# Attention kernel on one core: softmax denominators turned through 32x32 blocks before they are inverted

## The chip, the cores and the metric

The program runs on one core of a Trainium2 chip. The metric is the device time of one launch, in microseconds. PE is TensorE, DVE VectorE, ACT ScalarE, POOL GpSimd, SP the queue that issues most DMAs.

## What is computed

`x` is (2, 2048, 512), fp32. A layer norm of it goes into a causal attention with 16 heads of 32 and ALiBi slopes, and into a top-1 mixture of 8 experts; both are added to `x`. The change touches only the end of the softmax:

```python
attn = jnp.einsum('bhqd,bhkd->bhqk', q, k) / math.sqrt(HEAD_DIM)
attn = attn + alibi_bias(seq_len, N_HEADS)[None] + causal_mask(seq_len)[None, None]
attn = jax.nn.softmax(attn, axis=-1)
y = jnp.einsum('bhqk,bhkd->bhqd', attn, v)
...
x = x + _L0_attn_ref(xn, W_qkv, W_o) + _L0_ffn_ref(xn, wg, W, b)
```

The kernel divides late: it forms the unnormalised products with v and the row sums of the exponentials, and multiplies the one by the inverse of the other.

## The kernel before

Four stages follow each other, each in a block of its own that all engines enter and leave together: projection and routing (0 to about 360 us), attention (to 1560), the experts (to 1724), and the output product with the sums (to 1825). The change is in attention, function `attend`.

**Tiling.** Two batch rows of 16 heads make G = 8 groups of four heads (HG = 4), each head on 32 of the 128 partitions. A group's 2048 queries are QC = 4 chunks of 512. A round is one chunk with one block of 128 keys, up to the diagonal: 4 + 8 + 12 + 16 = NR = 40 rounds in a group. The last rounds of the chunks (LAST_ROUND) are 3, 11, 23 and 39.

**PE, lines 1131 to 1151.** PE goes through the rounds in pairs. For each pair it first issues eight score matmuls (L1082, four heads by two rounds; on diagonal rounds a small mask matmul at L1085 follows each), and between them the matmuls of the maxima (L1050): one max unit behind each score, four units in a round in the steady state. Here this is called a score stretch. Then come the value products (L1126) and row sums (L1117, L1093) of the pair of rounds before, here a value stretch, written to `y_ps` and `den_ps`, the two banks of `acc_ps`. The row sums use an all-ones matrix with 32 columns, so that the 32 partitions of a head all hold the same denominators. Each round's values raise `pv_done`. At the first round of a chunk the value stretch waits until the accumulators of the chunk before have left (L1101). Between two groups no value stretch stands between rounds 0-1 and 2-3: their scores form one double stretch.

**Maxima.** The row maxima are found ahead of the exponentials, some of them in the group before, by a hand-made plan (`PLAN_FIRST` for the first group, which has more units in a round, `PLAN_MID` for the six groups in the middle, `PLAN_LAST` for the last, which has none after round 14). DVE takes each max unit out of one of three banks of `max_ps` (L940, on the diagonal L936); PE needs a bank again three units later. FOLD, TURN and SPLIT make a chunk's maxima into rows: DVE L948, PE L1070, ACT L997, DVE L955; then SP stores them (L832).

**ACT.** Exponentials, L1021, out of three banks of `score_ps`. Two rounds after a chunk's last one ACT copies both banks of `acc_ps` into `acc_sb` (`leave`, L1005) and raises `accs_left`.

**DVE's inversion.** `den_sb` is the half of `acc_sb` with the denominators. `INVERT_AT` puts a quarter of it (128 columns) at the end of DVE's work for each of the rounds LAST_ROUND + 3 to + 6 (L972), in place. Chunk 3's fall into the next group's rounds 2 to 5.

**POOL.** Adds pairs of `probs` (L917) for the row sums, and multiplies `y_sb` by `den_sb` (`normalise`, L897) ahead of the pair that `Y_BEFORE_PAIR` names (pairs 1, 2, 5 and 9 of the 12). SP stores the product (L837); in the first group it stands ahead of the load of the second group's q and k (L804) in SP's order:

```python
y_out(g, 0)
max_rows(g, 2, half)
load(g + 1, 1 - half)
```

After the last group each engine runs the inversion of the last chunk with nothing else to do, and the block ends when the last `y` is stored.

Of the kernel before, what the change touches and what calls it, by code (L numbers as in the profile page):

```python
# [8 lines left out]
F32 = mybir.dt.float32  # L9
# [3 lines left out]
ACT = mybir.ActivationFunctionType  # L13
# [3 lines left out]
P = 128  # L17
B, S, D = 2, 2048, 512
H, DH = 16, 32
E = 8  # L20
N = B * S
CH = 512
# [8 lines left out]
QC = S // CH  # L31
# [19 lines left out]
NR = len(ROUNDS)  # L51
# [10 lines left out]
NPAIR = len(PAIR_OF) // 2  # L62
PAIR_LAST = {p: r for r, p in PAIR_OF.items()}
LAST_ROUND = [max(r for r, (cc, _) in enumerate(ROUNDS) if cc == c) for c in range(QC)]
# [73 lines left out]
def plan_of(g, last):  # L138
# [3 lines left out]
    if isinstance(g, int) and g == 0:  # L142
# [4 lines left out]


LEAVE_AT = {(LAST_ROUND[c] + 2) % NR: ((LAST_ROUND[c] + 2) // NR, c) for c in range(QC)}
QUARTERS = 4  # L150
INVERT_AT = {(LAST_ROUND[c] + 3 + k) % NR: ((LAST_ROUND[c] + 3 + k) // NR, c, k)
             for c in range(QC) for k in range(QUARTERS)}

Y_BEFORE_PAIR = {min([p for p in range(NPAIR) if PAIR_LAST[p] > (LAST_ROUND[c] + 3 + QUARTERS) % NR] or [NPAIR]):
                 ((LAST_ROUND[c] + 3 + QUARTERS) // NR, c) for c in range(QC)}


class Memory:
# [3 lines left out]
def wait_past(eng, sem, count):  # L162

    if not isinstance(count, int) or count > 0:
        eng.wait_ge(sem, count)
# [570 lines left out]
def attend(nc, m):  # L736
# [6 lines left out]
    with ExitStack() as c:  # L743
        sb = lambda n, s, d: c.enter_context(nc.sbuf_tensor(n, s, d))
# [9 lines left out]
        max_lo = sb("max_lo", [HG * TPC, 2, P], F32R)  # L754
        acc_sb = sb("acc_sb", [P, 2, 2, CH], F32)
        y_sb, den_sb = acc_sb[:, :, 0], acc_sb[:, :, 1]
        score_ps = pb("score_ps", [P, S_BANKS, CH], F32)
        max_ps = pb("max_ps", [P, M_BANKS, CH], F32)
        acc_ps = pb("acc_ps", [P, 2, CH], F32)
# [36 lines left out]
        with nc.Block() as block:  # L796
# [86 lines left out]
            @block.gpsimd  # L883
            def _(pool):
                nc.gpsimd.iota(token[:], [[P, NT]], base=0, channel_multiplier=1).then_inc(token_made, 1)  # L885
                pool.wait_ge(token_made, 1)

                def place_tokens(k):

                    for t in range(k * SCATTERS, (k + 1) * SCATTERS):  # L890
                        pool.indirect_dma_start(m.slot_token_d, bass.IndirectOffsetOnAxis(ap=m.slot_cell[:, t:t + 1], axis=0),
                                                token[:, t:t + 1], None).then_inc(tokens_stored, 16)

                def normalise(g, cc):
                    n = g * QC + cc
                    pool.wait_ge(inverted, (n + 1) * QUARTERS)
                    nc.gpsimd.tensor_tensor(y_sb[:, cc % 2], y_sb[:, cc % 2], den_sb[:, cc % 2], ALU.mult).then_inc(y_done, 1)  # L897

                def step(g, half, first, last):
                    exps, used = base(pool, g, NSU), base(pool, g, NPAIR)  # L900
                    for p in range(NPAIR + 1):
                        if p in Y_BEFORE_PAIR:
                            back, cc = Y_BEFORE_PAIR[p]
                            if not (first and back):
                                normalise(g - back, cc)
                        if p == NPAIR:
                            break
                        if first and 1 <= p <= NT // SCATTERS:
                            place_tokens(p - 1)
                        r1 = PAIR_LAST[p]  # L910
                        s0, s1 = (r1 - 1) % P_SLOTS, r1 % P_SLOTS
                        if not (first and p < 2):

                            pool.wait_ge(pair_used, used + (p - 1))
                        for hh in range(HG):
                            pool.wait_ge(exp_done, exps + (r1 * HG + hh + 1))
                            nc.gpsimd.tensor_tensor(pair_sum[:, p % 2, hh], probs[:, s0, hh], probs[:, s1, hh],  # L917
                                                    ALU.add).then_inc(pair_added, 1)

                groups(pool, step)  # L920
                normalise(G - 1, QC - 1)
                pool.wait_ge(tokens_stored, 16 * NT)

            @block.vector
            def _(dve):
                nc.vector.memset(neg_max[:], 0.0).then_inc(max_blank, 1)
                dve.wait_ge(max_blank, 1)
                part = part_max[:].rearrange("p (h i) k -> p h i k", h=HG)

                def take_max(u, bank, units):  # L930
                    i, kc, hh = MAX_UNITS[u]
                    w = min(CH, (i + 1) * P - kc * CH)
                    dve.wait_ge(max_scored, units + (u + 1))
                    if kc == i // TPC:

                        nc.vector.tensor_tensor_reduce(max_ps[:, bank, 0:w], max_ps[:, bank, 0:w], m.mask_row[:, CH - w:CH],  # L936
                                                       1.0, LOWEST, ALU.add, ALU.max,
                                                       part_max[:, hh * QT + i, kc:kc + 1]).then_inc(max_taken, 1)
                    else:
                        nc.vector.tensor_reduce(part_max[:, hh * QT + i, kc:kc + 1], max_ps[:, bank, 0:w], AX.X,  # L940
                                                ALU.max).then_inc(max_taken, 1)

                def fold(g, cc, units):

                    n = g * QC + cc
                    dve.wait_ge(max_taken, units + (OF_CHUNK[cc][-1] + 1))
                    wait_past(dve, max_turned, n)
                    nc.vector.tensor_reduce(neg_max[:, 0:HG * TPC].rearrange("p (h i) -> p h i", h=HG),  # L948
                                            part[:, :, cc * TPC:(cc + 1) * TPC, 0:cc + 1], AX.X, ALU.max,
                                            negate=True).then_inc(neg_done, 1)  # L950

                def low_rows(g, cc, bank):

                    dve.wait_ge(max_hi_done, g * QC + cc + 1)
                    nc.vector.tensor_tensor(max_lo[:, cc % 2], max_ps[0:HG * TPC, bank, 0:P], max_hi[:, cc % 2].bitcast(F32),  # L955
                                            ALU.subtract).then_inc(max_lo_done, 1)

                def maxima(events, banks, g, units):

                    for dg, kind, n in events:  # L960
                        if kind == UNIT:
                            take_max(n, banks[dg, kind, n][0], units[dg])
                        elif kind == FOLD:
                            fold(g + dg, n, units[dg])
                        elif kind == SPLIT:
                            low_rows(g + dg, n, banks[dg, TURN, n][0])

                def invert(g, cc, k):

                    dve.wait_ge(accs_left, g * QC + cc + 1)  # L970
                    quarter = den_sb[:, cc % 2, bass.ts(k, CH // QUARTERS)]
                    nc.vector.reciprocal(quarter, quarter).then_inc(inverted, 1)  # L972

                def step(g, half, first, last):
                    events, banks = plan_of(g, last)
                    units = base(dve, g, NMU), None if last else base(dve, g + 1, NMU)
                    for r in range(NR):
                        maxima(events[r], banks, g, units)
                        if r in INVERT_AT:
                            back, cc, k = INVERT_AT[r]  # L980
                            if not (first and back):
                                invert(g - back, cc, k)

                maxima(PLAN_BEFORE[0], BANKS_BEFORE, 0, (0, None))
                groups(dve, step)
                for k in range(QUARTERS):
                    invert(G - 1, QC - 1, k)

            @block.scalar
            def _(act):  # L990
# [9 lines left out]
                def leave(g, cc):  # L1000

                    act.wait_ge(pv_done, g * NR + LAST_ROUND[cc] + 1)

                    wait_past(act, y_stored[cc % 2], 16 * (g * (QC // 2) + cc // 2))
                    nc.scalar.activation(acc_sb[:, cc % 2], acc_ps[:], ACT.Copy).then_inc(accs_left, 1)  # L1005

                def step(g, half, first, last):
                    events, banks = plan_of(g, last)
# [25 lines left out]
            def _(pe):  # L1034
# [62 lines left out]
                def probs_of(g, r, exps):  # L1097
                    cc, jb = ROUNDS[r]
                    if jb == 0:

                        wait_past(pe, accs_left, g * QC + cc)  # L1101
                    pe.wait_ge(exp_done, exps + (r + 1) * HG)

                def has_row_sums(r):
# [370 lines left out]
```

## Time and profile before

| | us |
|---|---|
| median of 3 runs | 1824.9 |
| lowest, highest | 1824.75, 1836.62 |
| the profiled execution | 1827.11 |
| its span | 1825.4 |
| PE busy | 1687.3 (92%) |
| DVE busy | 1104.7 (61%) |
| ACT busy | 785.2 (43%) |
| POOL busy | 675.6 (37%) |

The profiled execution's own time is 1.7 us above its span and 2.2 us above the median. Busy shares are unions of the instructions of an engine; PE's matmuls overlap each other, so its 92% doesn't say how close it is to its best. The mean granted clock of TensorE over the span is 0.97.

### The profile page before, as it was taken

To read this page: it belongs to the slowest core of one execution; us is meant where nothing else is said; L and a number is where in the kernel's file an instruction comes from. 1 tells how busy PE (TensorE), PEld (TensorE's weight loads), DVE (VectorE), ACT (ScalarE), POOL (GpSimd) and SP (SyncE) were. 2 spreads that over 40 slices of the span, in tenths; PEclk is the share of its full clock that TensorE was granted. 3 is DMA by queue.
4 is the path that set the end of the run, shared out by engine and by line. 5 is a ranking of instruction groups with operands and counts; after the bars stand their busy time and mean duration, and the time that the engine had idled before them with its cause. 6 is when DMAs were issued, how large, how long until landed. Compare 5 with 4: busy or idle time off the path is not lost. (4 is left out here: it accounts for less than half of the span.)

```text
span 1825.4 us, 27949 instructions
## 1 busy us (share of the span) xinstructions
PE 1687.3 (92%) x9970; PEld 1015.6 (56%) x9971; DVE 1104.7 (61%) x2484; ACT 785.2 (43%) x1575; POOL 675.6 (37%) x643
## 2 busy tenths in 40 slices
PE   5999999579899999999999999999999999689898
PEld 4777777444444444454545444444554443568686
DVE  5333333468677767776876876876777710634466
ACT  2222222024354555564655555565556555411111
POOL 4500000006572552553444454355256256132360
PEclk9999999769999999999999999999999999899899
DMA  6655554744604503602701800900900500355596
GB/s 219 210 185 179 197 189 160 159 77 84 106 8 92 98 13 73 117 7 60 136 7 39 156 8 20 175 8 8 180 16 7 197 7 6 133 161 166 176 393 231
DMA packets 96927, 203.59 MB, mean 112 GB/s; under 512 B 10908, under 2 KB 28348, under 8 KB 91164
## 3 DMA queue, kind: packets, MB, share of 16 engines
q1 hardware_dynamic: 87592, 178.56, 37.8%
q0 software_dynamic: 9216, 23.47, 4.1%
q8 instruction: 72, 1.18, 0.3%
q14 instruction: 47, 0.39, 0.1%
HBM read 122.46 MB, written 79.01 MB: 110 GB/s over the span
## 5 line engine op out<-in xcount | busy, mean ns | idle before, releaser
L1021 ACT ACTIVATE probs_sb<-score_ps 128x512 f32<-128x512 f32 (+3 forms) x1280 | 606.8, 546 | 503.2 <-PE score_ps L1085 196.0
L917 POOL TENSOR_TENSOR pair_sum<-probs_sb 128x512 f32<-128x512 f32 x384 | 480.2, 1283 | 598.7 <-ACT probs_sb L1021 493.1
L940 DVE TENSOR_REDUCE part_max<-max_ps 128x1 f32<-128x512 f32 x768 | 474.2, 680 | 250.4 <-PE max_ps L1050 247.8
L1050 PE MATMUL max_ps<-k_aug,q_aug 104*128 104x512 f32 (+3 forms) x1280 | 534.1, 427 | 54.1 <-DMA q_aug<-q_rows_d 22.8
L1082 PE MATMUL score_ps<-q_aug,k_aug 106*128 106x512 f32 (+3 forms) x1280 | 494.3, 393 | 18.7 <-DMA q_aug<-max_lo 9.8
L1082 PEld LDWEIGHTS score_ps<-q_aug,k_aug 106*128 106x128 f32 x1280 | 243.7, 191 | 183.1 <-issue 112.1
L1050 PEld LDWEIGHTS max_ps<-k_aug,q_aug 104*128 104x128 f32 x1280 | 251.1, 197 | 160.7 <-DVE part_max L940 82.1
L1126 PE MATMUL acc_ps<-probs_sb,v_sb 128*32 128x512 f32 (+3 forms) x2560 | 294.6, 539 | 0.0
L936 DVE CUSTOM_DVE_ANT_0 max_ps<-max_ps,mask_row 128x384 f32<-128x384 f32 (+3 forms) x512 | 238.9, 515 | 57.1 <-PE max_ps L1050 55.6
L972 DVE RECIPROCAL acc_sb<-acc_sb 128x128 f32<-128x128 f32 x128 | 119.7, 940 | 76.6 <-ACT acc_sb L1005 76.6
L1126 PEld LDWEIGHTS acc_ps<-probs_sb,v_sb 128*32 128x32 f32 x2560 | 73.2, 110 | 117.4 <-issue 97.4
L613 DVE SCALAR_TENSOR_TENSOR st_lo<-group_ps,st_hi 128x512 fp32r<-128x512 f32 x64 | 44.3, 692 | 139.2 <-ACT st_hi L660 139.2
L1085 PE MATMUL score_ps<-mask_kq,ident_bf 128*128 128x128 bf16 x512 | 118.9, 232 | 0.0
L723 PE MATMUL group_ps<-xT_hi,w_hi 128*128 128x512 f32 x256 | 102.0, 398 | 0.0
L1093 PE MATMUL acc_ps<-pair_sum,ones 128*32 128x512 f32 x768 | 101.3, 599 | 0.0
L723 PE MATMUL group_ps<-xT_lo,w_hi 128*128 128x512 f32 x256 | 101.3, 396 | 0.0
L723 PE MATMUL group_ps<-xT_hi,w_lo 128*128 128x512 f32 x256 | 101.2, 395 | 0.0
L660 ACT ACTIVATE st_hi<-group_ps 128x512 fp32r<-128x512 f32 x64 | 38.3, 598 | 141.1 <-PE group_ps L723 141.1
L885 POOL IOTA token<- 128x32 int32 x1 | 0.2, 154 | 256.4 <-POOLq L346 256.4
L1117 PE MATMUL acc_ps<-probs_sb,ones 128*32 128x512 f32 (+3 forms) x1024 | 93.7, 438 | 0.0
L1085 PEld LDWEIGHTS score_ps<-mask_kq,ident_bf 128*128 128x128 bf16 x512 | 50.0, 98 | 76.5 <-issue 58.4
L1224 POOL DMA_INDIRECT rows<-xn_d,slot_token x39 | 37.3, 957 | 97.6 <-PE turn_ps L1321 90.2
(173 smaller groups left out, 1737.8 us busy)
## 6 DMA issues: line engine op xcount, KB each, us to landing
k_aug<-k_hi_d SPq DMA_DIRECT2D x14, 1024.0 KB
q_aug<-q_hi_d SPq DMA_DIRECT2D x14, 1024.0 KB
slot_y_d<-y_rows SPq DMA_DIRECT2D x39, 256.0 KB, 2.0
xn_d<-xn SPq DMA_DIRECT2D x8, 1024.0 KB, 5.5
q_hi_d<-st_hi SPq DMA_DIRECT2D x32, 256.0 KB, 3.4
q_lo_d<-st_lo SPq DMA_DIRECT2D x32, 256.0 KB, 3.7
k_hi_d<-st_hi SPq DMA_DIRECT2D x32, 256.0 KB, 2.5
k_lo_d<-st_lo SPq DMA_DIRECT2D x32, 256.0 KB, 2.8
```

The lines of the kernel that those rows point to most:

```text
L723: last = nc.tensor.matmul(group_ps[:, n % BANKS], lhs, rhs, start=(k == 0 and p == 0), stop=(k == KC - 1 and p == 2))
L917: nc.gpsimd.tensor_tensor(pair_sum[:, p % 2, hh], probs[:, s0, hh], probs[:, s1, hh], ALU.add).then_inc(pair_added, 1)
L936: nc.vector.tensor_tensor_reduce(max_ps[:, bank, 0:w], max_ps[:, bank, 0:w], m.mask_row[:, CH - w:CH], 1.0, LOWEST, ALU.add, ALU.max, part ...
L940: nc.vector.tensor_reduce(part_max[:, hh * QT + i, kc:kc + 1], max_ps[:, bank, 0:w], AX.X, ALU.max).then_inc(max_taken, 1)
L972: nc.vector.reciprocal(quarter, quarter).then_inc(inverted, 1)
L1021: nc.scalar.activation(probs[:, r % P_SLOTS, hh, off:CH], score_ps[:, (r * HG + hh) % S_BANKS, off:CH], ACT.Exp).then_inc(exp_done, 1)
L1050: nc.tensor.matmul(max_ps[:, bank, 0:w], q_aug[0:ROW_MAX, half, hh, i * P:(i + 1) * P], k_aug[0:ROW_MAX, half, hh, kc * CH:kc * CH + w], s ...
L1082: last = nc.tensor.matmul(score_ps[:, u % S_BANKS, off:CH], k_aug[0:ROWS, half, hh, jb * P:(jb + 1) * P], q_aug[0:ROWS, half, hh, cc * CH ...
L1085: last = nc.tensor.matmul(score_ps[:, u % S_BANKS, off:off + P], m.ident_bf[:], m.mask_kq[:], start=False, stop=True)
L1093: last = nc.tensor.matmul(den_ps[hh * DH:(hh + 1) * DH, :], m.ones[:], pair_sum[:, p % 2, hh], start=start, stop=False)
L1117: nc.tensor.matmul(den_ps[hh * DH:(hh + 1) * DH, off:CH], m.ones[:], probs[:, r % P_SLOTS, hh, off:CH], start=jb == 0, stop=r == LAST_ROUN ...
L1126: last = nc.tensor.matmul(y_ps[hh * DH:(hh + 1) * DH, off:CH], v_sb[:, half, jb, hh * DH:(hh + 1) * DH], probs[:, r % P_SLOTS, hh, off:CH] ...
```

## The change

The inversion has three steps in place of four quarters. Step 0, at round LAST_ROUND + 2, transposes `den_ps` straight out of PSUM in blocks of 32 x 32 into `den_sb`: after it partition i of a head holds query 32 s + i in each column of block s. Step 1, a round later, takes one column of each of the 16 blocks (16 elements a partition, step 32) and inverts those into `den_fold`. Step 2, another round later, reads `den_fold` with each element repeated 32 times, transposes again in 32 x 32 blocks, and leaves the inverses of all 512 queries on all 32 partitions of a head in `den_sb`. Each step waits for the one before it; step 0 also waits for `pv_done` of the chunk's last round and for `y_done` of two chunks earlier. ACT copies only the `y_ps` bank, 512 columns. POOL waits for `accs_left` too, and goes ahead of pairs 1, 2, 4 and 8. PE, at the first value products of a chunk, waits for step 0 of the chunk before in addition to `accs_left`.

```diff
-QUARTERS = 4
-INVERT_AT = {(LAST_ROUND[c] + 3 + k) % NR: ((LAST_ROUND[c] + 3 + k) // NR, c, k)
-             for c in range(QC) for k in range(QUARTERS)}
+INVERT_STEPS = 3
+INVERT_AT = {(LAST_ROUND[c] + 2 + k) % NR: ((LAST_ROUND[c] + 2 + k) // NR, c, k)
+             for c in range(QC) for k in range(INVERT_STEPS)}
...
+        den_fold = sb("den_fold", [P, CH // DH], F32)
...
-                    pool.wait_ge(inverted, (n + 1) * QUARTERS)
+                    pool.wait_ge(accs_left, n + 1)
+                    pool.wait_ge(inverted, (n + 1) * INVERT_STEPS)
...
-                    dve.wait_ge(accs_left, g * QC + cc + 1)
-                    quarter = den_sb[:, cc % 2, bass.ts(k, CH // QUARTERS)]
-                    nc.vector.reciprocal(quarter, quarter).then_inc(inverted, 1)
+                    n = g * QC + cc
+                    if k == 0:
+                        dve.wait_ge(pv_done, g * NR + LAST_ROUND[cc] + 1)
+
+                        wait_past(dve, y_done, n - 1)
+                        nc.vector.transpose(den_sb[:, cc % 2], den_ps).then_inc(inverted, 1)
+                    elif k == 1:
+
+                        dve.wait_ge(inverted, n * INVERT_STEPS + 1)
+                        nc.vector.reciprocal(den_fold[:], den_sb[:, cc % 2].rearrange("p (s d) -> p s d", d=DH)[:, :, 0]).then_inc(
+                            inverted, 1)
+                    else:
+                        dve.wait_ge(inverted, n * INVERT_STEPS + 2)
+                        nc.vector.transpose(den_sb[:, cc % 2].rearrange("p (s d) -> p s d", d=DH),
+                                            den_fold[:].unsqueeze(2).to_broadcast([P, CH // DH, DH])).then_inc(inverted, 1)
...
-                for k in range(QUARTERS):
+                for k in range(INVERT_STEPS):
                     invert(G - 1, QC - 1, k)
...
-                    nc.scalar.activation(acc_sb[:, cc % 2], acc_ps[:], ACT.Copy).then_inc(accs_left, 1)
+                    nc.scalar.activation(y_sb[:, cc % 2], y_ps, ACT.Copy).then_inc(accs_left, 1)
...
                         wait_past(pe, accs_left, g * QC + cc)
+                        wait_past(pe, inverted, (g * QC + cc) * INVERT_STEPS - INVERT_STEPS + 1)
```

## Rows read from the trace of the kernel before

**Rows 1.** Busy time by engine, one middle group of attention (stretch first, then us)

```profile
713.00:854.00 141.00, 136.69 (x936) 69.73 (x930) 103.73 (x248) 79.64 (x168) 65.04 (x52) 1.00 0.35 66
```

**Rows 2.** Waits in that group: waiter <- releaser: us, times, longest

```profile
ACT probs_sb L1021 <- POOL pair_sum L917: 17.1, 6, 3.5
...
PE max_ps L1050 <- DVE part_max L936: 1.8, 3, 0.7
...
PE max_ps L1050 <- DVE part_max L940: 1.3, 2, 0.8
...
PE score_ps L1082 <- ACT probs_sb L1021: 0.6, 2, 0.5
PE max_ps L1050 <- DVE max_lo L955: 0.3, 1, 0.3
```

**Rows 3.** DVE's timeline, a middle group (start us, us, instructions)

```profile
874.18 2.48 DVE L940 TENSOR_REDUCE part_max<-max_ps 128x1 f32<-128x512 f32 x4 [0.63 <-PE max_ps L1050]
876.58 0.94 DVE L972 RECIPROCAL acc_sb<-acc_sb 128x128 f32<-128x128 f32 x1
877.44 2.41 DVE L940 TENSOR_REDUCE part_max<-max_ps 128x1 f32<-128x512 f32 x4
```

**Rows 4.** ACT's timeline: its copy at the start of rounds 6-7 of that group

```profile
873.54 1.03 ACT L1005 ACTIVATE acc_sb<-acc_ps 128x1024 f32<-128x1024 f32 x1 [1.82 <-PE acc_ps L1126]
```

**Rows 5.** PE's timeline: rounds 4-5 of that group, and the next stretch's wait

```profile
867.10 0.50 PE L1082 MATMUL score_ps<-q_aug,k_aug 106*128 106x512 f32 x1
...
871.65 0.39 PE L1050 MATMUL max_ps<-k_aug,q_aug 104*128 104x256 f32 x1 [0.62 <-DVE part_max L936]
871.97 0.64 PE L1117 MATMUL acc_ps<-probs_sb,ones 128*32 128x256 f32 x8
...
878.12 0.50 PE L1050 MATMUL max_ps<-k_aug,q_aug 104*128 104x512 f32 x1 [0.55 <-DVE part_max L940]
```

**Rows 6.** PE's timeline: rounds 30-31 of that group

```profile
958.25 0.50 PE L1082 MATMUL score_ps<-q_aug,k_aug 106*128 106x512 f32 x1
...
962.27 1.06 PE L1126 MATMUL acc_ps<-probs_sb,v_sb 128*32 128x512 f32 x8
```

**Rows 7.** Groups of instructions by line: busy us, mean ns, idle before

```profile
L940 DVE TENSOR_REDUCE part_max<-max_ps 128x1 f32<-128x512 f32 x768 | 474.2, 680 | 250.4 <-PE max_ps L1050 247.8 <-issue 2.3
...
L972 DVE RECIPROCAL acc_sb<-acc_sb 128x128 f32<-128x128 f32 x128 | 119.7, 940 | 76.6 <-ACT acc_sb L1005 76.6
...
L1005 ACT ACTIVATE acc_sb<-acc_ps 128x1024 f32<-128x1024 f32 x32 | 32.8, 1025 | 40.4 <-PE acc_ps L1126 40.4
...
L665 ACT ACTIVATE st_v<-group_ps 128x512 f32<-128x512 f32 x32 | 19.1, 597 | 70.7 <-PE group_ps L723 70.7
...
L488 DVE RECIPROCAL inv<-root 128x4 f32<-128x4 f32 x8 | 1.4, 178 | 43.3 <-ACT root L637 43.3
```

**Rows 8.** PE's timeline: rounds 14-15 of the same group

```profile
904.21 0.50 PE L1082 MATMUL score_ps<-q_aug,k_aug 106*128 106x512 f32 x1 [0.45 <-ACT probs_sb L1021]
```

**Rows 9.** SP's timeline in the first group

```profile
432.44 0.36 SPq L837 DMA_DIRECT2D y_d<-acc_sb  x1
```

**Rows 10.** DVE's timeline in the first group

```profile
430.12 0.94 DVE L972 RECIPROCAL acc_sb<-acc_sb 128x128 f32<-128x128 f32 x1
```

**Rows 11.** PE's timeline in the first group: one wait for DVE

```profile
427.87 0.50 PE L1050 MATMUL max_ps<-k_aug,q_aug 104*128 104x512 f32 x1 [0.71 <-DVE part_max L940]
```

**Rows 12.** PE's timeline in the first group: its wait for the second group's rows

```profile
481.43 0.47 PE L1050 MATMUL max_ps<-k_aug,q_aug 104*128 104x128 f32 x1 [3.45 <-DMA q_aug<-q_rows_d]
```

**Rows 13.** All engines' timeline at the end of attention

```profile
1551.62 1.02 ACT L1005 ACTIVATE acc_sb<-acc_ps 128x1024 f32<-128x1024 f32 x1 [5.06 <-PE acc_ps L1126]
1552.67 3.39 DVE L972 RECIPROCAL acc_sb<-acc_sb 128x128 f32<-128x128 f32 x4 [42.16 <-ACT acc_sb L1005]
1556.14 1.26 POOL L897 TENSOR_TENSOR acc_sb<-acc_sb 128x512 f32<-128x512 f32 x1 [14.47 <-DVE acc_sb L972]
...
1560.38 14.80 PE L1311 MATMUL turn_ps<-ident,w_nat 128*128 128x128 f32 x110 [8.82 <-PEq L796]
```

More of the change, by code:

```diff
@@ L149 @@
 LEAVE_AT = {(LAST_ROUND[c] + 2) % NR: ((LAST_ROUND[c] + 2) // NR, c) for c in range(QC)}
-QUARTERS = 4
-INVERT_AT = {(LAST_ROUND[c] + 3 + k) % NR: ((LAST_ROUND[c] + 3 + k) // NR, c, k)
-             for c in range(QC) for k in range(QUARTERS)}
-Y_BEFORE_PAIR = {min([p for p in range(NPAIR) if PAIR_LAST[p] > (LAST_ROUND[c] + 3 + QUARTERS) % NR] or [NPAIR]):
-                 ((LAST_ROUND[c] + 3 + QUARTERS) // NR, c) for c in range(QC)}
+INVERT_STEPS = 3
+INVERT_AT = {(LAST_ROUND[c] + 2 + k) % NR: ((LAST_ROUND[c] + 2 + k) // NR, c, k)
+             for c in range(QC) for k in range(INVERT_STEPS)}
+Y_BEFORE_PAIR = {min([p for p in range(NPAIR) if PAIR_LAST[p] > (LAST_ROUND[c] + 2 + INVERT_STEPS) % NR] or [NPAIR]):
+                 ((LAST_ROUND[c] + 2 + INVERT_STEPS) // NR, c) for c in range(QC)}
 class Memory:
```

## The prediction

> **What bounds the kernel now.** I read the page first, then the windows of attention, the waits of one group, and the timelines of PE, DVE and ACT inside it. Attention takes about two thirds of the time and repeats with a period of 141 us; in one such group PE is busy for 136.7 of 141 us, DVE for 103.7, ACT for 79.6 [rows 1]. So PE sets the period, and only what makes PE stop can give time back. The reader should see in the waits which stops there are: PE stood for DVE's maxima 1.8 us (3 times), 1.3 (2 times) and 0.3 (once), and for ACT's exponentials 0.6 us [rows 2]. 4.0 us of 141 is the most direct part of what a lighter DVE and ACT can return.
>
> DVE is not slow on average, yet it is within a score stretch. A max unit of 512 columns costs it about 0.60 us in sequence (2.48 us for four, overlapping), and PE issues one with each score about every 0.50 us (eight in 4.02 us [rows 6]). With three banks DVE can fall behind by two units before PE stops. Where a reciprocal stands between the fourth and the fifth unit it adds 0.86 us (876.58 to 877.44) [rows 3], and PE's last max of the stretch starts after a stop of 0.55 us; in rounds 4-5 it is 0.62 us [rows 5]. Each chunk has four reciprocals. Those of its first and third round lie inside stretches; the other two lie at the end of a stretch, where PE goes on to value products, and cost nothing.
>
> What a stop costs is more than its idle row. Rounds 4-5 and rounds 30-31 hold the same matmuls (eight scores of 512 columns, four max units of 512 and four of 256), and only the first has a reciprocal inside: 867.10 to 871.97 is 4.87 us [rows 5], 958.25 to 962.27 is 4.02 us [rows 6]. The difference is 0.85 for an idle row of 0.62, so I add 0.23 us a stop.
>
> **What the change removes and adds on DVE.** Removed: 128 reciprocals of 128 columns, 940 ns each, 119.7 us in all [rows 7], 3.76 us a chunk. Added a chunk: one reciprocal of 16 columns and two transposes of 512. The reciprocal's price follows from two sizes: 178 ns for 4 columns, 940 for 128, so 6.15 ns a column and 0.25 us for 16 [rows 7]. No row shows a transpose. The nearest is DVE's pass over 512 columns of PSUM, 680 ns (L940 [rows 7]); I take 0.69 us for both, since each moves 512 columns once. Below, the trace has no DVE pass over 512 columns that takes less than 0.60 us in sequence (2.41 us for four [rows 3]); above, the dearest column in the trace is the reciprocal's, 6.15 ns, which would make 3.3 us. Between ends so far apart I go by the L940 row, as a transpose does no arithmetic. A chunk then costs DVE 0.69 + 0.25 + 0.69 = 1.63 us, 2.1 less; over 32 chunks DVE loses about 68 us of work. Most of it is under PE's work and worth nothing; what counts is where the pieces lie.
>
> The third step reads one word 32 times over and the second steps by 32 words. The Trainium skill (Vector Engine (DVE) Microarchitecture Reference, Measured stream behaviour on trn2) says that a port keeps its full rate only for runs of at least two adjacent words, and gives 1.7 to 2.5 ns a column for streams that jump at every element. No run here shows that for a transpose; by it the third step would be an estimated 0.3 to 0.8 us longer, and as that step lies under value products the sum would change by that once, at the end of attention.
>
> **Where the new steps lie, in a middle group.** Chunks 0, 1 and 2 end in an odd round L. Step 0 follows the max units of round L+2, the end of a stretch, and waits for `pv_done` of L, which comes with the end of the value stretch behind it: ACT's copy, which waits for the same, starts at 873.54 [rows 4], and DVE's first unit of the next stretch would start at 874.18 [rows 3]. Behind the waiting step stand only that unit and its followers, which PE has not issued yet, so the wait is free; the transpose runs to about 874.25 and delays them by 0.1 us. Step 1 lies inside that stretch and adds 0.2 us in sequence where there were 0.86. Step 2 lies at the stretch's end, hidden under the value products, where 0.94 us of reciprocal is hidden now. The stretch after that has nothing.
>
> - Second stretches (rounds 4-5, 8-9, 16-17, 28-29): the three stops for L936, 1.8 us [rows 2], plus 3 x 0.23, go: 2.5 us.
> - First stretches: rounds 6-7, 0.55 [rows 5] + 0.23, less the 0.3 that the new steps add: 0.5. Rounds 26-27, the 0.3 for max_lo + 0.23, less about 0.15: 0.35. Rounds 14-15 are held by ACT, whose copy of 1025 ns comes ahead of the exponentials (PE stops for 0.45 us [rows 8]); 512 columns cost it 597 ns [rows 7], so 0.4 comes back.
> - Chunk 3's steps fall into the double stretch of rounds 0-3, step 0 after round 1 and step 1 after round 2: 0.94 us inside it, as before. Step 1 and step 0 cost 0.2 and 0.7 in sequence, and step 0 comes where DVE has room before its next unit; I take 0.25.
>
> Together 2.5 + 1.5 = 4.0 us a group, 24 us for six groups.
>
> **The added waits of PE and POOL.** PE's wait for step 0 is read at the value products, more than 4 us into the stretch [rows 5, 6]; step 0 ends 0.9 us into it. Free, with 3 us to spare. POOL's `normalise` comes a pair earlier for three chunks of four, and its inputs are ready by then; it stops waiting for the fourth reciprocal. SP's stores follow earlier. None of this is late for anyone. If that cover went, POOL's 1.3 us would hold back pair sums, for which ACT already waited 17.1 us a group as the last of its conditions [rows 2].
>
> **The last group.** Rounds 0 to 9 as before: 0.25 + 0.85 + 0.5 + 0.75 = 2.3 us. After that there are no maxima and DVE is idle; ACT's shorter copies give 0.4 and 0.3. At the very end nothing covers: ACT's copy at 1551.62, the reciprocals from 1552.67 for 3.39 us, POOL at 1556.14, and PE's first expert work at 1560.38 [rows 13]. The new chain starts at 1551.62 beside ACT's copy and takes 0.69 + 0.25 + 0.69 plus two handovers of some 0.05: POOL starts at 1553.4, 2.7 us sooner. Sum 5.7 us.
>
> **The first group.** SP can only load the second group's rows after `y` of chunk 0 is stored, at 432.44, and after eight stores of maxima rows that follow 0.4 us later [rows 9]. PE later waits 3.45 us for that load [rows 12]. Now `y` would be out well before, since chunk 0's inverses are ready by round 7 in place of round 9. The maxima rows then wait for `max_lo` of chunk 2 alone. It starts at the end of a reciprocal, 430.12 + 0.86 [rows 10]; that reciprocal goes (0.9), and the stretches before it shrink by 0.45 and by 0.71 [rows 11] + 0.23, so it is ready near 428.9. The load is issued 3.9 us sooner. PE itself arrives at its wait some 2.7 us sooner, so the wait persists and the whole 3.9 us is passed on. Chunk 2's two stretches behind it give 0.4 and 0.9. Sum 5.2 us.
>
> **Sum.** 24 + 5.7 + 5.2 = 34.9 us. On the profiled execution's span of 1825.4 (own time 1827.11, 2.2 above the median) that is 1790.5; on the median of 1824.9 it gives 1790.0.
>
> **The rivals.**
> - *Transposes at half the pass rate.* A 4-byte word through a 32 x 32 block may take two passes: 1.2 to 1.3 us each. Nothing in the trace speaks for or against. Step 0 then delays the three first stretches by 0.55 more and adds as much in the double stretch; those gains vanish (1.5 to about 0 and -0.3), the 2.5 stay, the end gives 1.6. 2.2 x 6 + 3.4 + 4.5 = 21: 1804.
> - *The stops move.* ACT serves three banks too, and ACT itself waits for POOL [rows 2]. If PE, released by DVE, stops for these instead, only half of the middle groups' gain and the ends remain: 12 + 8 = 20 or less, down to 12: about 1809. Against it: rounds 30-31 run in 4.02 us with the same ACT and POOL work.
> - *Slower.* The transposes cost like the reciprocal, per column (3.3 us). Step 0, at the head of a stretch, holds back every max unit by whatever it takes above 0.6 us, in all 32 chunks, and a step 2 that outlasts the value products (taken as 1.4 us) holds back the next stretch too. The group's gain of 4.0 is 1.0 a chunk, so the change breaks even at about 1.5 us a transpose; 1% slower needs about 1.9; at 3.3 us it is about 3.5 us a chunk lost: 1930.
> - *More comes back.* The new steps add nothing inside a stretch: all idle rows and 0.23 for each of eight stops go, 4.0 + 1.8 = 5.8 us a group [rows 2]: 35 + 6 + 6 = 47: 1778.
>
> **Chances and range.** The forecast has 0.62, half rate 0.12, moved stops 0.12, slower 0.05, more 0.09. Within 1% (18.2 us, about what a measurement can tell from no change) lie half of moved stops, a third of half rate and some of the miss of the forecast: 0.14. Faster by over 1%: 0.81. Slower by over 1%: 0.05. The range takes in half rate and most of more: 1780 to 1808.
>
> **What would show it.** The transposes' mean under 0.75 us, the small reciprocal near 0.25; the first unit of rounds 6-7 starting within 0.15 us of where it did; the waits PE <- L936 and L940 of a group down from 3.1 us to under 1.2; rounds 4-5 at 4.0 us; the group's period 137.2; the second group's load issued near 434; PE's first expert transpose 2.7 us nearer to the end of the values. Transposes above 1.5 us, or a period within 1 us of 141, would make the prediction wrong.

## The result, and the profile after

Over four runs of each on one chip the changed kernel took 1799.2 us (1796.28 to 1800.37), the one before 1825.33 (1824.75 to 1836.62): a ratio of 0.9833, 95% interval 0.9805 to 0.9862. That is 26 us less, where 34.9 had been forecast. The profiled executions have spans of 1798.0 and 1825.4, 27.4 apart. Busy times of the engines, from the page of the kernel after:

```profile
PE 1684.9 (94%) x9970; PEld 1020.1 (57%) x9971; DVE 1041.0 (58%) x2452; ACT 774.4 (43%) x1575; POOL 675.3 (38%) x643
```

DVE lost 63.7 us of work and ACT 10.8. Where the 27.4 us lie, read from the starts of score matmuls in PE's timeline (a group's period is the distance from its first one to the next group's; the first group is counted from its rounds 4-5, whose first score starts at 406.60 and 406.42):

| part of the kernel | before | after | gain | forecast |
|---|---|---|---|---|
| first group, from its rounds 4-5 | 165.57 | 154.28 | 11.3 | 5.2 |
| six middle groups, period of one (mean) | 141.27 | 139.35 | 1.9, x6 = 11.5 | 4.0, x6 = 24 |
| last group, to the first score of its rounds 38-39 | 123.94 | 122.16 | 1.8 | 3.0 |
| from there to the first expert matmul | 16.66 | 14.03 | 2.6 | 2.7 |
| all else | | | 0.2 | 0 |

So the total is near the forecast with two errors in it of opposite sign: the middle groups gave less than half of what they should, the first group twice as much.

**The new instructions.** Three views by source line, kernel after (ns min/median/max, first and last start in us, form), and ACT's copy:

```profile
L977 DVE STREAM_TRANSPOSE acc_sb<-acc_ps x32: 710/716/718, 413.6 to 1526.9; 128x512 f32<-128x512 f32 x32
L981 DVE RECIPROCAL den_fold<-acc_sb x32: 231/243/254, 416.8 to 1527.6; 128x16 f32<-128x16 f32 x32
L985 DVE STREAM_TRANSPOSE acc_sb<-den_fold x32: 689/701/711, 419.9 to 1527.9; 128x512 f32<-128x512 f32 x32
L1019 ACT ACTIVATE acc_sb<-acc_ps x32: 592/597/600, 413.6 to 1526.9; 128x512 f32<-128x512 f32 x32
```

They cost what was taken: 716, 243 and 701 ns against 0.69, 0.25 and 0.69 us.

**Their place in rounds 6-7**, DVE's timeline after (start, us):

```profile
855.82 0.72 DVE L977 STREAM_TRANSPOSE acc_sb<-acc_ps 128x512 f32<-128x512 f32 x1 [0.80 <-PE acc_ps L1141]
856.46 2.48 DVE L942 TENSOR_REDUCE part_max<-max_ps 128x1 f32<-128x512 f32 x4
858.86 0.24 DVE L981 RECIPROCAL den_fold<-acc_sb 128x16 f32<-128x16 f32 x1
859.02 2.41 DVE L942 TENSOR_REDUCE part_max<-max_ps 128x1 f32<-128x512 f32 x4
861.35 0.70 DVE L985 STREAM_TRANSPOSE acc_sb<-den_fold 128x512 f32<-128x512 f32 x1
```

The small reciprocal stands where [rows 3] has the one of 0.94 us; the fifth unit follows it by 0.16 us, not 0.86. The stretch's first score starts at 855.68, so the first unit starts 0.78 us into it.

**The middle group, stretch by stretch.** Length of the score stretches in the group of [rows 1], PE's timelines:

| rounds | before | after | gain | forecast |
|---|---|---|---|---|
| 0-3 | 9.26 | 8.77 | 0.49 | 0.25 |
| 4-5 | 4.87 | 4.03 | 0.84 | 0.85 |
| 6-7 | 5.14 | 4.44 | 0.70 | 0.5 |
| 8-9 | 5.19 | 4.47 | 0.72 | 0.7 |
| 14-15 | 4.37 | 7.41 | -3.04 | 0.4 |
| 16-17 | 4.83 | 4.02 | 0.81 | 0.9 |
| 26-27 | 5.33 | 4.75 | 0.58 | 0.35 |
| 28-29 | 4.07 | 3.90 | 0.17 | 0 |

Every stretch that DVE had held gained; one that the forecast had gaining 0.4 lost 3.0. This group's period went from 141.27 to 140.02.

**What happens in rounds 14-15.** PE's timeline after, then ACT's:

```profile
883.35 0.50 PE L1096 MATMUL score_ps<-q_aug,k_aug 106*128 106x512 f32 x1
...
887.22 0.80 PE L1096 MATMUL score_ps<-q_aug,k_aug 106*128 106x512 f32 x1 [2.62 <-ACT probs_sb L1035]
...
890.76 1.92 PE L1141 MATMUL acc_ps<-probs_sb,v_sb 128*32 128x512 f32 x16
```

```profile
886.08 0.60 ACT L1019 ACTIVATE acc_sb<-acc_ps 128x512 f32<-128x512 f32 x1 [3.89 <-DMA y_d<-acc_sb]
886.58 2.07 ACT L1035 ACTIVATE probs_sb<-score_ps 128x512 f32<-128x512 f32 x4
```

PE fills its three score banks and stops for 2.62 us for ACT; ACT stands in front of its copy of chunk 1, and what it waits for is neither PE nor POOL but a store of `y`: `y_stored[1]`, raised by the store of chunk 3 of the group before, which had the same slot. SP's timelines, after and then before:

```profile
838.43 0.35 SPq L805 DMA_DIRECT2D k_aug<-k_hi_d  x1
...
842.56 0.40 SPq L823 DMA_DIRECT2D v_sb<-v_d  x1
850.43 30.88 SPq L838 DMA_DIRECT2D y_d<-acc_sb  x2
```

```profile
854.82 0.35 SPq L804 DMA_DIRECT2D k_aug<-k_hi_d  x1
...
876.65 20.55 SPq L837 DMA_DIRECT2D y_d<-acc_sb  x2
```

Each row of two (x2) is the store of chunk 3 and, right behind it, that of this group's chunk 0, whose own issue takes under 0.7 us. Both kernels issue the store of chunk 3 behind the nine DMAs that load the next group's q, k and v, and in both SP stays in that one issue until the load has moved far enough: to 880.6 after, to 896.7 before. The issue starts 26.2 us earlier, but it ends only 16.1 us earlier, as the load itself (838.43 against 854.82) began 16.4 earlier. The windows show the load's end (stretch, length, busy us of PE, PEld, DVE, ACT, POOL, granted clock, DMA share, GB/s); before first, then after:

```profile
900.00:902.00 2.00, 2.00 (x24) 1.05 (x27) 2.00 (x7) 1.34 (x3) 2.00 (x2) 1.00 0.29 110
902.00:904.00 2.00, 1.76 (x26) 1.21 (x18) 1.65 (x8) 1.36 (x2) 2.00 (x3) 1.00 0.00 0
```

```profile
884.00:886.00 2.00, 0.60 (x4) 0.30 (x2) 1.07 (x8) 0.00 (x0) 1.79 (x2) 1.00 0.31 116
886.00:888.00 2.00, 0.78 (x4) 0.69 (x4) 0.00 (x0) 1.92 (x4) 0.00 (x0) 0.80 0.01 2
```

The transfers end some 47 us after the load's first issue in both. After, the store's landing is recorded: 47.6 us behind that issue in this group, 46.3 to 47.6 in the six middle groups. For the kernel before no landing of a store is recorded; its transfers end just ahead of 902.6, when ACT's copy started, released by PE and not by a store:

```profile
902.64 1.02 ACT L1005 ACTIVATE acc_sb<-acc_ps 128x1024 f32<-128x1024 f32 x1 [1.30 <-PE acc_ps L1126]
```

From the load's issue to this copy there were 47.8 us of PE's work before. The gains of rounds 0 to 9, 2.75 us together, cut that to 45.1, and the load did not get faster. If the stores of before landed like those of after, the wait had 0.2 to 1.5 us of slack (an estimate: 47.8 less 47.6 and 46.3). The view by source line of SP's stores, after, has who waited for them and their landing times:

```profile
  ACT acc_sb L1019: 18.5, 6
...
DMA to landing us min/median/max: 2.4/2.6/35.6
```

Six waits, one in each middle group, 18.5 us. PE's stops behind them are 1.80, 1.32, 2.62, 1.82, 1.52 and 1.85 us, 1.8 on average.

### The profile page after: what moved, and what is told of

Read it like the earlier page. It is cut to its first block and busy times, and to the rows that moved or that the text cites. A ratio compares the mean times of both kernels' runs of the same rounds, so it can differ in the third digit from the quotient of the medians.

```text
span 1798.0 us, 27979 instructions
## 1 busy us (share of the span) xinstructions
PE 1684.9 (94%) x9970; PEld 1020.1 (57%) x9971; DVE 1041.0 (58%) x2452; ACT 774.4 (43%) x1575; POOL 675.3 (38%) x643
## 5 line engine op out<-in xcount | busy, mean ns | idle before, releaser
L613 DVE SCALAR_TENSOR_TENSOR st_lo<-group_ps,st_hi 128x512 fp32r<-128x512 f32 x64 | 44.2, 691 | 139.3 <-ACT st_hi L660 139.2
L899 POOL TENSOR_TENSOR acc_sb<-acc_sb 128x512 f32<-128x512 f32 x32 | 41.2, 1287 | 180.6 <-DVE acc_sb L985 180.6
```

## The experiments

**Three slots for y, each with its own semaphore.** The store stays where it is; what ACT's copy waits for becomes a chunk older. The denominators have one slot in place of two, so step 0 waits for the product of the chunk just before.

```diff
-        acc_sb = sb("acc_sb", [P, 2, 2, CH], F32)
-        y_sb, den_sb = acc_sb[:, :, 0], acc_sb[:, :, 1]
+        y_sb = sb("y_sb", [P, 3, CH], F32)
+        den_sb = sb("den_sb", [P, 1, CH], F32)
...
-                    wait_past(act, y_stored[cc % 2], 16 * (g * (QC // 2) + cc // 2))
+                    wait_past(act, y_stored[n % 3], 16 * (n // 3))
```

> The changed kernel with three slots for y in place of two (each with its own semaphore) and one for the denominators, so that ACT's copy of chunk 1 waits for the store of the group before's chunk 2, not chunk 3. Theory A (chunk 3's y store lies in the same DMA queue behind the 8 MB load of the next group, lands about 47.7 us after that load's first issue, and holds ACT's copy, by 2.6 us and by the half clock behind it): the stop before ACT's copy at rounds 14-15 goes, the period of a middle group falls from 139.35 to about 135.9 us, the time to about 1779. Theory B (POOL's earlier normalise delays the pair sums, the store has nothing to do with it): the period stays at 139.35 and the time at 1799.

Measured: 1782.93 us, ratio 0.9738 (0.9709 to 0.9766). SP's timeline and the view of its stores by source line show that the store is as late as ever:

```profile
851.11 29.57 SPq L839 DMA_DIRECT2D y_d<-y_sb  x1
...
DMA to landing us min/median/max: 2.4/2.8/35.3
```

but ACT's copy is released by PE, and PE does not stop (ACT's and PE's timelines, same group):

```profile
884.16 0.60 ACT L1021 ACTIVATE y_sb<-acc_ps 128x512 f32<-128x512 f32 x1 [1.30 <-PE acc_ps L1143]
...
884.02 0.50 PE L1098 MATMUL score_ps<-q_aug,k_aug 106*128 106x512 f32 x1
...
887.89 1.50 PE L1143 MATMUL acc_ps<-probs_sb,v_sb 128*32 128x512 f32 x12
```

Rounds 14-15 take 3.87 us in place of 7.41, and the six periods are 136.4 to 136.5. Against the 139.35 of the kernel after that is 2.9 us a group: the wait for the store took 17.5 us of the change's gain away. And without that wait the change is worth 4.8 us a group (141.27 - 136.44), not 4.0.

**The store issued by POOL**, right behind `normalise`, so that it isn't on the queue of the load.

```diff
-                    sp.dma_start(m.y_d[...], y_sb[:, cc % 2]).then_inc(y_stored[cc % 2], 16)
...
+                    pool.wait_ge(y_done, n + 1)
+                    pool.dma_start(m.y_d[...], y_sb[:, cc % 2]).then_inc(y_stored[cc % 2], 16)
```

> The changed kernel with y stored by POOL through its own queue right after normalise, not by SP. Theory A, in the form that a store waits only behind what is ahead of it in its own queue: it lands within 10 us of its issue though the load is under way, the stop goes, the period is 136 to 137 us (POOL spends about 0.85 us more a chunk), the time about 1781. Theory C (the 16 DMA engines are busy with the load and any store lands behind it): the stop stays near 2.6 us and the time near 1799. Theory B: 1799 or more.

Measured: 1785.59 us, 0.9757 (0.9727 to 0.9787), period 136.43. The view of ACT's copies by source line has PE as the only one they waited for (us, times):

```profile
  PE acc_ps L1142: 34.4, 25
```

So the store is in time, though the load runs as before. Its landing is not recorded in this run; the control below has it. The queue it is, and not the store's own cost. At the end of attention the POOL-issued store comes later (17.5 us in place of 14.0).

**POOL multiplies where it did before.** After, with the pairs of `Y_BEFORE_PAIR` as in the kernel before. The rival here was that the earlier store, or POOL's place, is the cause.

```diff
-Y_BEFORE_PAIR = {min([p for p in range(NPAIR) if PAIR_LAST[p] > (LAST_ROUND[c] + 2 + INVERT_STEPS) % NR] or [NPAIR]):
+Y_BEFORE_PAIR = {min([p for p in range(NPAIR) if PAIR_LAST[p] > (LAST_ROUND[c] + 7) % NR] or [NPAIR]):
```

> The changed kernel with POOL's normalise back ahead of pairs 1, 2, 5 and 9. Theory A (landing set by the load in front in the queue, not by when the store is issued): y of chunk 3 is issued some 5 us later, lands at the same 47.7 us after the load's issue, stop and period stay (139.35 us), time 1798 to 1801. Theory B (POOL's positions): the stop goes, period about 136 us, and the two value stretches of 4.1 us in the last group go back to 2.7: about 1777.

Measured: 1807.49 us, 0.9884 (0.9847 to 0.9921), period 138.97. The wait stays, in all six groups (tile view of `y_d`, who waited):

```profile
  ACT acc_sb L1019: 17.2, 6
```

So the store issued later is not on time either, as the load sets its landing. My number for this kernel was wrong by 6 us for another reason: in the profiled execution its first group took 163.56 us, 9.3 more than after's, with long stretches at TensorE's lower clock (last section).

**The old reciprocals, only moved.** The kernel before, its four reciprocals a chunk put two and two at the ends of stretches. No transpose, DVE's work as before.

```diff
-INVERT_AT = {(LAST_ROUND[c] + 3 + k) % NR: ((LAST_ROUND[c] + 3 + k) // NR, c, k)
-             for c in range(QC) for k in range(QUARTERS)}
+INVERT_AT = {(LAST_ROUND[c] + 4 + k) % NR: ((LAST_ROUND[c] + 4 + k) // NR, c, k)
+             for c in range(QC) for k in (0, 2)}
...
                                 invert(g - back, cc, k)
+                                invert(g - back, cc, k + 1)
```

> The kernel before with the same four reciprocals of 128 columns, but two of them at the end of round L+4 and two at the end of L+6, so that none lies inside a score stretch. Theory P (it is the place of DVE's work that costs, not its amount): the stops of 0.5 to 0.8 us in rounds 4-5, 6-7, 8-9 and 16-17 go or shrink, though two reciprocals (1.8 us) outlast the shortest value stretches by up to 0.9 us; what is gained before round 14 is given back at ACT's copy, which then waits for the y store as in the changed kernel; 1808 to 1816. Theory Q (the 2.1 us of DVE work a chunk is what counts): no gain, 1825.

Measured: 1813.66 us, 0.9908 (0.9876 to 0.994), period 139.66. The stretches are those of the kernel after (4.03, 4.38, 4.46, 4.03, 4.67 and 3.88 us in rounds 4-5, 6-7, 8-9, 16-17, 26-27 and 28-29), and the same new wait appears. ACT's timeline:

```profile
894.98 1.02 ACT L1006 ACTIVATE acc_sb<-acc_ps 128x1024 f32<-128x1024 f32 x1 [3.32 <-DMA y_d<-acc_sb]
```

**Moved, and stored by POOL.** Both edits above, on the kernel before.

> The kernel before with two reciprocals at the end of round L+4 and two at L+6, ACT copying both banks, and y stored by POOL, so that neither a stop inside a stretch nor the late store is left: what of the gain needs the transposes. Theory P (place, not amount): period 136.5 to 137.2 us, only ACT's longer copy (about 0.5 us a group) and the uncovered end (2.7 us) left to the transposes, time 1790 to 1797. Theory Q (amount): period above 139 us, time above 1808.

Measured: 1797.39 us, 0.9814 (0.9767 to 0.9861), period 136.41. That is the period of the three-slot kernel, with none of the change in it. Here the whole gain of the middle groups is that nothing of 0.86 us stands between two max units any more; that DVE does 2 us less a chunk is worth nothing there. The two kernels are not equal stretch by stretch: rounds 14-15 take 4.29 us here, with ACT's long copy, against 3.87, and rounds 0-3 take 8.45, with no transpose, against 8.77. What the change gains by ACT's copy it gives back by its own steps. DVE's timeline shows where the reciprocals lie:

```profile
857.49 1.76 DVE L973 RECIPROCAL acc_sb<-acc_sb 128x128 f32<-128x128 f32 x2
```

What it lacks against 1782.93 lies outside them: first group 161.88 against 158.57, last 122.6 against 118.6, end of attention 20.13 against 14.03, where nothing covers the reciprocals or POOL's store. The total is 0.4 us above what I expected.

**The control: the kernel before, stored by POOL.**

> Control: the kernel before with y stored by POOL as in e3 and nothing else. Theory A (in the kernel before the store of chunk 3 lands just ahead of ACT's copy and holds nobody): middle groups keep 141.3 us, the end of attention grows by the 3.5 us seen in e3, time 1824 to 1834. If the store's path were worth something by itself, the period would fall below 141.

Measured: 1832.51 us over ten runs, 1.0032 (1.0013 to 1.0052), period 141.23 (141.27 before). The view of POOL's stores by source line has the landing that the run above lacks:

```profile
DMA to landing us min/median/max: 2.7/3.5/13.3
```

In the middle groups the recorded stores of chunk 3, issued by POOL at 878.2 and the like with the load under way, landed 11.4 to 13.3 us later; those without a load beside them took 2.7. So they share the DMA engines with the load but don't stand behind all of it. Where ACT does not wait for the store, its earlier landing gives nothing, and the end of attention loses 3.5 us. So the 2.9 us a group exist only once DVE's stops are gone.

**Step 0 done twice**, on the three-slot kernel: it puts a known 0.72 us at the head of a stretch.

```diff
+                        nc.vector.transpose(den_sb[:, 0], den_ps).then_inc(twice, 1)
+                        dve.wait_ge(twice, n + 1)
                         nc.vector.transpose(den_sb[:, 0], den_ps).then_inc(inverted, 1)
```

> The kernel with three y slots and step 0 done twice in a row, 1.43 us in place of 0.72 at the head of a stretch. It prices a slower transpose. Theory A (above 0.69 us each further us at the head of a stretch costs PE as much): the period grows by 2.0 to 2.8 us, the time to 1796 to 1801. Theory E (DVE's lag is made good within the stretch): period within 0.5 us of 136.4, time 1783 to 1786.

Measured: 1804.88 us, 0.9849 (0.9801 to 0.9898), period 138.96, 2.5 more. DVE's timeline, a stretch that starts with the two:

```profile
866.28 0.72 DVE L979 STREAM_TRANSPOSE den_sb<-acc_ps 128x512 f32<-128x512 f32 x1 [0.80 <-PE acc_ps L1146]
867.03 0.72 DVE L981 STREAM_TRANSPOSE den_sb<-acc_ps 128x512 f32<-128x512 f32 x1
867.67 2.44 DVE L944 TENSOR_REDUCE part_max<-max_ps 128x1 f32<-128x512 f32 x4
```

The stretch starts at 866.15, so the first max unit starts 1.52 us into it in place of 0.78, and rounds 0-3, 6-7 and 26-27 grow by 0.75, 0.71 and 0.73; rounds 14-15, with less DVE work, by 0.25. A step 0 of 1.4 us would thus have cost some 2.5 us a group, 15 us in the six. So the price of step 0, which no row of before showed, was a figure on which the prediction hung as much as on the missed wait. The total is 4 us above what I expected: in the profiled execution the first group took 3.1 us and the last 4.8 us more than in the three-slot kernel.

**ACT copies twice**, on the three-slot kernel: ACT reads the `y_ps` bank once more, into a scratch tile `den_copy` (bf16), which gives back about the length of the copy's removed half.

```diff
+                    nc.scalar.activation(den_copy[:], y_ps, ACT.Copy).then_inc(den_copied, 1)
                     nc.scalar.activation(y_sb[:, n % 3], y_ps, ACT.Copy).then_inc(accs_left, 1)
```

> The kernel with three y slots, in which ACT copies the y bank twice (first into a scratch tile, then into its slot), about 1.1 us in place of 0.6. It prices ACT's part of the change alone. Theory A (ACT's copy ahead of the exponentials is on the path at rounds 14-15 and 26-27, elsewhere covered): the score stretch of rounds 14-15 grows from 3.87 to about 4.3 us, the period from 136.4 to about 137.0, the last group by 0.7, the time to 1786 to 1789. Theory D (all of the change's gain is DVE's): no change, 1783.

Measured: 1792.35 us (1783.58 to 1794.5), 0.9792 (0.9746 to 0.9839); its runs lie in two clusters, about 1784 and 1793, and the profiled one is of the lower. There the period is 136.94, 0.5 more; rounds 14-15 take 4.34 in place of 3.87 and PE stops again:

```profile
882.63 0.50 PE L1100 MATMUL score_ps<-q_aug,k_aug 106*128 106x512 f32 x1 [0.52 <-ACT probs_sb L1039]
```

That is the 0.45 of [rows 8]: ACT's shorter copy is worth 0.5 us a group, in that stretch and no other. Why the runs fall into two clusters stays open, and with it why the median is above the 1786 to 1789 that I expected.

**Step 1 at the end of a stretch, in front of step 2**, on the three-slot kernel: nothing of the inversion is left between max units.

```diff
-             for c in range(QC) for k in range(INVERT_STEPS)}
+             for c in range(QC) for k in (0, 2)}
...
+                                if k == 2:
+                                    invert(g - back, cc, 1)
                                 invert(g - back, cc, k)
```

> The kernel with three y slots and step 1 moved to the end of round L+4, just ahead of step 2, so that nothing but the transpose at the head is left in a stretch. Theory A: 0.17 us of DVE less inside the stretches of rounds 0-3, 6-7 and 26-27, at most 0.5 us a group: period 135.9 to 136.4, time 1779 to 1783. If the reciprocal of 16 were free there: 1783.

Measured: 1780.41 us, 0.9726 (0.9678 to 0.9773), period 136.25 against 136.44. It is the lowest of the complete kernels, but its time can't be told from the three-slot one; the period, even in all six groups, says that the 0.24 us cost 0.1 in rounds 0-3 and 0.1 in 6-7.

**No transposes at all**, on the three-slot kernel. DVE inverts 16 columns straight from `den_ps` where step 0 was, steps 1 and 2 are left out, and POOL multiplies `y` by itself, so what it computes is not the attention.

> The kernel with three y slots in which both transposes are left out: DVE only inverts 16 columns straight from PSUM, POOL multiplies y by itself, so the output is not the normalised one. It bounds what DVE's steps still cost in the middle groups. Theory A (the step at the head of a stretch still holds DVE's first unit, as doubling it cost its full 0.72 us): the period falls from 136.4 by 0.2 to 1.0 us, the time to 1775 to 1782. If the transposes were fully hidden: 136.4.

Measured: 1774.07 us, 0.9719 (0.9677 to 0.9761), period 135.86. All that the new steps still cost a middle group is 0.6 us, and the end of attention 1.4.

## Why the prediction was right, and which of its steps were not

- **The bound, and the price of the three steps: right.** PE's stops for DVE were what a lighter DVE could return, and [rows 7] priced steps it did not show to within 0.03 us. Step 2, which repeats each word 32 times, took 701 ns; step 0, which reads its words in order but out of PSUM, took 716. By the rule on jumping streams of the Trainium skill (Vector Engine (DVE) Microarchitecture Reference, Measured stream behaviour on trn2) step 2 would have been an estimated 0.3 to 0.8 us longer; here the measurement decides against it.
- **Gain inside the stretches: right in kind, 4.0 where 4.8 was measured.** The second stretches came out to 0.1 us. Undersized were the first ones, as I charged the new steps against them with 0.3 and 0.15 and they cost 0.1 in each (4.45 and 4.75 us against 4.34 and 4.68 without transposes): 0.70 for 0.5, 0.58 for 0.35, and 0.49 for 0.25 in rounds 0-3. The 0.4 for ACT's copy was 0.5. The last piece, 0.17 in rounds 28-29, I had at nothing. The rival "more comes back", by which the new steps add nothing at all, has 5.8 us a group; the runs lie between the two.
- **"None of this is late for anyone": wrong.** This is the step that failed. I asked what the added waits and the earlier stores hold up, and not which existing wait had no slack left. ACT's copy of chunk 1 waits for the store of chunk 3, that store stands behind a load of 47 us, and only 47.8 us of PE's work lay between. In the trace of before the wait did not exist: its copy was released by PE. It cost 1.8 us a group of stopped PE and 1.1 beyond the stop, where the lower clock lies, 17.5 us in all. The three-slot kernel, where ACT's copy waits for an older store, has neither.
- **A wrong row in front of it.** My description of the change puts POOL's multiplications ahead of pairs 1, 2, 4 and 8; they stand ahead of 0, 2, 4 and 8, in place of 1, 2, 5 and 9. With pair 0, chunk 3's `y` is multiplied at 849.13 and its store is issued at 850.43, early in the load. It did not decide the case: with the old places the wait stays.
- **The rival "the stops move": part of it came true.** PE, released by DVE, does stop for ACT. But I had ACT waiting for POOL; it waits for a DMA, and in one stretch only. The forecast's mechanism and this rival's both acted, and the sum of the middle groups, 11.5 us, is the rival's 12.
- **First group: 11.3 us for 5.2.** The steps that I worked out came about: `y` was stored at 426.07, the second group's load was issued at 433.73, 4.1 us sooner (3.9 forecast), and PE's wait for it ended at 476.64 in place of 481.43. SP's timeline and PE's, after:

```profile
426.07 0.36 SPq L838 DMA_DIRECT2D y_d<-acc_sb  x1
...
433.73 0.44 SPq L805 DMA_DIRECT2D k_aug<-k_hi_d  x1
...
476.64 0.33 PE L1064 MATMUL max_ps<-k_aug,q_aug 104*128 104x128 f32 x1 [1.83 <-DMA q_aug<-q_rows_d]
```

  The rest, 6.1 us, was not in my sum, which had nothing of the clock in it. Behind PE's wait for the load the clock fell in both kernels, for longer before: up to round 26 the group gained 6.1 us, not 3.9. And before, rounds 26 to 29 ran in part at the lower clock: they took 21.2 us there and 16.0 after, 5.2 for the forecast's 1.3.
- **Last group: 1.8 for 3.0.** Two value stretches of it ran at the lower clock after (4.16 and 4.12 us in place of 2.71); in the three-slot kernel, which has none there, it gained 5.3. Of that 1.1 is clock too, as before had one such value stretch, behind rounds 14-15 (2.98 in place of 1.85).
- **End of attention: right.** 2.6 for 2.7. The chain of [rows 13] is now:

```profile
1527.63 0.25 DVE L981 RECIPROCAL den_fold<-acc_sb 128x16 f32<-128x16 f32 x1
1527.92 0.71 DVE L985 STREAM_TRANSPOSE acc_sb<-den_fold 128x512 f32<-128x512 f32 x1
1528.78 1.26 POOL L899 TENSOR_TENSOR acc_sb<-acc_sb 128x512 f32<-128x512 f32 x1 [11.84 <-DVE acc_sb L985]
```

- **The rival "slower": its sizes don't follow from its own prices.** With 1.0 us a chunk to give back, 1% slower needs about 1.8 us a transpose, not 1.9, and 3.3 us would give some 1940, not 1930. Nothing hangs on it.

The time came within 9 us of the forecast by luck: the shortfall of the middle groups, 12.5 us, was half made up by the clock in the first, 6.1. Without that it would have been about 1805, still inside the range, which takes in half rate (1804) and ends at 1808. The range had been drawn for other reasons; of my signs the price of the steps, rounds 4-5, the load at 433.7 and the end came true, and the period of 137.2 did not (139.35).

## What to carry to other kernels

Small work between the units of a stream that is itself the tightest costs most of its length where the engine has no room left (0.7 to 0.85 us for 0.72 to 0.94 here) and less where it has (0.1 for 0.24), and at the end of a stretch it costs nothing: moving the old reciprocals, with the store off SP's queue, gave the middle groups all that the new algorithm did. When stops are taken out of a loop, list every wait on a DMA whose length doesn't shrink with it, and compare the loop's new distance from issue to use with the DMA's: a wait that the trace doesn't show may be a microsecond away. A small store behind a large load on one queue lands with the load; a third buffer gave back 16 us of the whole here, another queue 14.

## What the runs showed of the hardware

**A store behind a load on SP's queue.** It landed up to 35.6 us after its issue, 2.4 where no load was ahead of it; SP stood in the issue for up to 30.8 us (kernel after). From POOL's queue, beside the same load, it was 11.4 to 13.3 us, and 2.7 with no load (the kernel before, stored by POOL). The Trainium skill (DMA: Bandwidth & Descriptors, Queues, rings and completion order) says that each DMA engine takes turns between the queues that have work for it; these times agree with that, as a store on a queue of its own gets its turns while the load goes on, and still has to share.

**The clock behind a short stop.** After most of PE's stops of rounds 14-15 the granted clock was at its lower level, 1.2 GHz, for a time. Windows of 8 us behind three of them, kernel after: the stop of 1.32 us, the one of 2.62, the one of 1.82.

```profile
747.00:755.00 8.00, 6.83 (x38) 4.00 (x38) 4.84 (x24) 6.31 (x14) 5.74 (x5) 1.00 0.02 5
...
887.00:895.00 8.00, 7.78 (x38) 5.04 (x38) 4.85 (x20) 5.93 (x13) 5.40 (x5) 0.79 0.02 5
1026.00:1034.00 8.00, 7.57 (x36) 4.55 (x37) 4.42 (x18) 5.54 (x13) 5.44 (x5) 0.79 0.01 2
```

A mean of 0.79 over 8 us is 1.7 us of full clock lost; not all of it shows in the time. The period of the group with the 1.32 us stop was 137.8, which is the 136.45 of the kernel without stops plus the stop itself. The five others lost 0.9 to 1.6 us beyond their stop (140.02 - 136.45 - 2.62 = 0.95 for the second shown; 139.3 - 136.45 - 1.82 = 1.0 for the third). So a stop cost its row plus 0.9 to 1.6 us where the clock followed, and the row alone where it didn't.

**The same in the first group and at the end.** Windows: before in rounds 26-29 of the first group, after in the last group, and the three-slot kernel and the one with POOL's old places in their first groups:

```profile
522.00:526.00 4.00, 4.00 (x21) 1.13 (x25) 2.62 (x6) 0.00 (x0) 0.78 (x1) 0.57 0.02 2
```

```profile
1457.00:1461.00 4.00, 4.00 (x22) 1.09 (x25) 0.00 (x0) 1.49 (x4) 1.16 (x1) 0.57 0.00 0
```

```profile
436.00:444.00 8.00, 7.90 (x45) 3.29 (x48) 2.52 (x11) 0.56 (x3) 0.00 (x0) 0.57 1.02 215
```

```profile
488.00:496.00 8.00, 7.45 (x36) 2.91 (x40) 4.41 (x15) 0.89 (x4) 0.00 (x0) 0.57 0.00 0
```

PE is busy in all four and slow in all four. In the last group of after no stop of PE over 0.31 us stands in the 15 us ahead of its window. In the first group every kernel has such stretches, in different places and numbers. Its time was 154.5 to 158.6 us in the three-slot kernel and the one with POOL's stores, and 163.6 with POOL's old places, more than these edits move in it. What decides where they fall was not settled: differences of under 10 us in the total between two of these kernels are not to be read as the edit's, and the middle groups' period, equal to 0.1 us over six groups in the kernels without the stop, is the better measure.
